# Gated cross-attention and routed experts on one core: the weights' low halves spread over the attention stage and beyond it, another order at the hand-off, and the second weight's exponential formed on ScalarE

## The chip, the cores and the metric
One Trainium2 chip, of which the kernel uses one core. The metric is the device time of one execution in microseconds (us); three executions of the kernel before took 288.73, 289.17 and 289.31, the median is 289.17. The profiled execution is a fourth.

## The reference
All in float32. x is 8 batches of 256 rows of 512; ctx is 8 batches of 256 rows of 512.

```python
def _layernorm(x): return (x - mean) / sqrt(var + 1e-5)

scores = einsum('bsd,bmd->bsm', layernorm(x), ctx) / sqrt(512)
scores = where(mask, scores, -1e30)
attn   = softmax(scores)
x = x + tanh(g_xattn) * where(any(mask), einsum('bsm,bmd->bsd', attn, ctx), 0)

xt    = layernorm(x).reshape(2048, 512)
probs = softmax(xt @ w_router.T)                # 8 experts
top_v, top_i = top_k(probs, 2); top_v /= sum(top_v)
g, u  = xt @ w_gate[e].T, xt @ w_up[e].T        # 192 columns each
out   = sum over the two experts of top_v * ((silu(g) * u) @ w_down[e].T)
x = x + tanh(g_ffn) * out
```

## The kernel before, in words
There are two stages on one core, with no pause between them.

**Attention.** The 2048 rows are cut into 16 tiles of 128 rows, numbered k, two per batch. A loop over steps s from 0 to 16 runs on every engine in the same form; each engine has its own queue, written out by hand, and semaphores join them. In step s TensorE transposes tile s (`t1`), transposes the attention weights of tile s-2 (`tp`), forms the scores of tile s-1 (`score`), the router's logits of tile s-4 (`rt`), the attention output of tile s-2 (`pv`) and transposes the second layernorm's output of tile s-3 (`t2`). VectorE in step s adds the attention output of tile s-3 to x (`x2`, the line X<-PO,rinv,X), takes the statistics of that sum, then those of the freshly loaded tile s+2 (`st1`), the row maximum of tile s-1 and the two bias columns. GpSimd raises the variances to the power -1/2 (`rstd`, rs<-mv) for both layernorms. ScalarE evicts, normalizes (XL and Y) and takes the exponentials.

Between these VectorE weaves the routing of each batch b: the two largest logits and their columns (`top2`), ranks among the rows of one expert (`ranks`), coefficients (`coefs`) and a table of slots (`slots`). Before, `top2` ends with dd = second maximum minus first, and `weigh` on ScalarE takes exp(dd).

**Weights.** 40 units of 128 by 512 or 64 by 512 numbers, numbered u: for expert e the parts n = 0, 1, 2 (gate and up), 3 (first 128 rows of down) and 4 (the last 64 rows of down). SyncE loads a unit (`loadw`), ScalarE rounds it to the high half (`hi`, semaphore s_wh), GpSimd subtracts to get the low half (`lo`, semaphore s_wl, the lines WGl<-WGl,WGh and so on). `SPLIT` says how many units each step takes. A unit with n = 4 is loaded into one of two buffers WS, so its load waits until the low half of the n = 4 unit two experts earlier is formed. SyncE's queue holds in one order the loads of x (`loadx`), of both forms of ctx (`loadct`, `loadcx`), of the weights and the stores of the routing coefficients: what stands behind a waiting load waits too.

**Experts.** The pairs (row, expert) are sorted by expert into 36 tiles of 128 rows that are run. The first NE = 9 of them come from batches 0 to 3 alone, so that their rows can be gathered before the attention is done. For tile j GpSimd gathers the rows (`gather`, XG<-x2s), TensorE transposes them (`tx`), multiplies with gate and up in three products of high and low halves (`gu`), transposes the product (`th`) and multiplies with down (`down`); ScalarE scales the result, and GpSimd scatters it with an addition into the output (out<-YT). `fence` and `landed` make a scatter wait for the one before it where the two may touch the same rows. TensorE waits before tile 0 until all 40 low halves are there.

## Time and profile before

| | |
|---|---|
| median of three executions | 289.17 us |
| the profiled execution | 288.54 us |
| its span, first to last instruction | 286.7 us |
| outside the span | 1.8 us |
| first `x2` of the attention starts | 18.50 us |
| last `x2` starts | 124.44 us |
| first expert product starts | 122.29 us |
| TensorE's mean granted clock | 0.973 |
| busy TensorE, VectorE, ScalarE, GpSimd | 87%, 62%, 52%, 58% |

A row of a timeline has the start and the duration in us, the engine and the line, then what is written from what, and in brackets the idle time of the engine before it with what ended it. Durations of neighbours on one engine overlap by about 0.1 us, since instructions are pipelined; the distance of two starts tells more than a sum of durations. A row of the windows has the stretch, its length, each engine's busy time with the number of instructions, the granted clock, the share in which the DMA engines were busy, and GB/s.

### The profile page before, as it was taken

To read this page: it belongs to the slowest core of one execution; us is meant where nothing else is said; L and a number is where in the kernel's file an instruction comes from. 1 tells how busy PE (TensorE), PEld (TensorE's weight loads), DVE (VectorE), ACT (ScalarE), POOL (GpSimd) and SP (SyncE) were. 2 spreads that over 40 slices of the span, in tenths; PEclk is the share of its full clock that TensorE was granted. 3 is DMA by queue.
4 is the path that set the end of the run, shared out by engine and by line. 5 is a ranking of instruction groups with operands and counts; after the bars stand their busy time and mean duration, and the time that the engine had idled before them with its cause. 6 is when DMAs were issued, how large, how long until landed. Compare 5 with 4: busy or idle time off the path is not lost.

```text
span 286.7 us, 5375 instructions
## 1 busy us (share of the span) xinstructions
PE 250.5 (87%) x1464; PEld 210.7 (73%) x1464; DVE 176.5 (62%) x645; ACT 149.9 (52%) x308; POOL 165.7 (58%) x153
## 2 busy tenths in 40 slices
PE   0999888988797878779999999999999999999940
PEld 0876666765575556459999889999999999999920
DVE  4465497999999799486586644454444454444420
ACT  3477977767585663154353445445445445444430
POOL 1267786567476465063632565648778875777440
PEclk9999999999999999798999999999999999999995
DMA  6999999988988321255543467459888999588753
GB/s 210 386 394 336 325 303 341 328 261 287 288 274 264 133 110 39 74 169 167 114 75 41 74 119 177 80 93 163 171 168 155 154 169 173 98 157 157 126 73 40
DMA packets 25951, 52.08 MB, mean 182 GB/s; under 512 B 5249, under 2 KB 5377, under 8 KB 25921
## 3 DMA queue, kind: packets, MB, share of 16 engines
q0 software_dynamic: 8304, 19.83, 37.8%
q1 hardware_dynamic: 13008, 23.50, 25.1%
q10 hardware_dynamic: 4608, 8.39, 7.7%
q8 instruction: 15, 0.25, 0.4%
q14 instruction: 16, 0.12, 0.2%
HBM read 33.81 MB, written 17.89 MB: 180 GB/s over the span
## 4 chain that ended last, share of the span: by engine, by line
PE 46%; DVE 21%; DMA 9%; issue 9%; POOL 8%; ACT 4%; ACTq 1%; POOLq 0%; DVEq 0%
PE S L1305 6%; PE S L1309 6%; PE S L1306 6%; DMA out<-YT,IXE 5%; PE A L1295 4%; DVE st L698 4%; PE PO L1154 3%; DVE X L739 3%; PE PO L1326 2%; PE PO L1331 2%; PE PO L1330 2%; PE PO L1327 2%; PE PO L1328 2%; DVE TB L805 2%; POOL WGl L407 2%
## 5 line engine op out<-in xcount | busy, mean ns | idle before, releaser
L1305 PE MATMUL S<-WGh,XTh 128*128 x144 | 52.1, 362 | 0.1
L1306 PE MATMUL S<-WGl,XTh 128*128 x144 | 48.8, 339 | 0.0
L398 POOL TENSOR_TENSOR rs<-mv,CS 128x1 f32<-128x1 f32 x32 | 17.8, 556 | 46.4 <-DVE mv L704 45.8
L492 POOL DMA_INDIRECT out<-YT,IXI x19 | 30.1, 1585 | 15.1 <-issue 5.7
L589 ACT ACTIVATE SG<-S 128x192 f32<-128x192 f32 x36 | 11.9, 332 | 49.0 <-PE S L1309 43.2
L1030 DVE TENSOR_TENSOR H<-SG,S 128x192 f32<-128x192 f32 x36 | 12.7, 354 | 39.7 <-ACT SG L589 34.7
L424 POOL DMA_INDIRECT XG<-x2s,IXG x30 | 29.5, 985 | 9.6 <-issue 5.5
L1154 PE MATMUL PO<-CX,PT 128*128 128x512 f32 x64 | 32.8, 637 | 2.5 <-DVE X L739 1.9
L407 POOL TENSOR_TENSOR WGl<-WGl,WGh 128x512 fp32r<-128x512 f32 x24 | 30.3, 1273 | 5.8 <-ACT WGh L570 5.6
L1309 PE MATMUL S<-WGh,XTl 128*128 x144 | 31.0, 337 | 0.0
L1143 PE MATMUL S<-CT,XLT 128*128 128x256 f32 x128 | 30.9, 385 | 0.0
L1023 DVE TENSOR_TENSOR XTl<-A,XTh 128x512 fp32r<-128x512 f32 x37 | 25.5, 690 | 8.1 <-ACT XTh L582 7.3
L582 ACT ACTIVATE XTh<-A 128x512 fp32r<-128x512 f32 x37 | 22.1, 599 | 11.3 <-PE A L1295 8.1
L1305 PEld LDWEIGHTS S<-WGh,XTh 128*128 128x128 f32 x144 | 27.5, 191 | 0.3 <-issue 0.2
L1306 PEld LDWEIGHTS S<-WGl,XTh 128*128 128x128 f32 x144 | 27.6, 192 | 0.0
L603 ACT ACTIVATE YT<-PO,cj 128x512 f32<-128x512 f32 x26 | 17.9, 688 | 17.7 <-PE PO L1331 13.1
L1036 DVE TENSOR_TENSOR HTl<-S,HTh 128x256 fp32r<-128x256 f32 x36 | 15.3, 424 | 18.7 <-ACT HTh L595 16.2
L1309 PEld LDWEIGHTS S<-WGh,XTl 128*128 128x128 f32 x144 | 25.6, 188 | 0.3 <-DVE XTl L1023 0.3
L1143 PEld LDWEIGHTS S<-CT,XLT 128*128 128x128 f32 x128 | 23.6, 195 | 2.9
L698 DVE BATCH_NORM_STATS2 st<-X 128x6 f32<-128x512 f32 x32 | 22.0, 689 | 4.3 <-DMA X<-in_x 3.6
L1295 PE MATMUL A<-CS,XG 128*128 128x128 f32 x148 | 22.7, 276 | 1.8 <-DMA XG<-x2s,IXE 1.7
L492 POOL DMA_INDIRECT out<-YT,IXE x7 | 11.2, 1594 | 19.1 <-DMA out<-YT,IXE 11.5
(168 smaller groups left out, 569.5 us busy)
## 6 DMA issues: line engine op xcount, KB each, us to landing
WGl<-in_wgu SPq DMA_DIRECT2D x24, 256.0 KB, 5.9
X<-in_x SPq DMA_DIRECT2D x16, 256.0 KB, 4.9
CT<-in_ctxt SPq DMA_DIRECT2D x8, 512.0 KB, 6.1
CX<-in_ctxn SPq DMA_DIRECT2D x8, 512.0 KB, 4.4
out<-X ACTq DMA_DIRECT2D x16, 256.0 KB, 4.9
x2s<-Y ACTq DMA_DIRECT2D x16, 256.0 KB, 3.9
WD1l<-in_wd SPq DMA_DIRECT2D x8, 256.0 KB, 5.4
WS<-in_wd SPq DMA_DIRECT2D x8, 256.0 KB, 5.3
```

The lines of the kernel that those rows point to most:

```text
L407: pool.tensor_tensor(out=low, in0=raw[p], in1=hi[p].bitcast(fp32), op=ALU.subtract).then_inc(s_wl, 1)
L424: pool.indirect_dma_start(out=XG[:, xg(j), :], out_offset=None, in_=rows, in_offset=bass.IndirectOffsetOnAxis(ap=at, axis=0))\
L492: pool.indirect_dma_start(out=out, out_offset=bass.IndirectOffsetOnAxis(ap=to, axis=0), in_=yt(j), in_offset=None, compute_op=ALU.add)\
L582: act.activation(XTh[:, j % 2, :, :], A0[:, :].rearrange("p (k c) -> p k c", k=KC), ACT.Copy).then_inc(s_xh, 1)
L698: n = mark(dve.bn_stats(st[:, k % 2, :], src))
L1023: dve.tensor_tensor(XTl[:, j % 2, :, :], A0[:, :].rearrange("p (k c) -> p k c", k=KC), XTh[:, j % 2, :, :].bitcast(fp32), ALU.subtract).th ...
L1143: m = pe.matmul(SC[k % 2][:, 0:S], XLT[:, k % 2, c, :], CT[:, b % 2, c, :], start=False, stop=(c == KC - 1))
L1154: m = pe.matmul(PO[:, :], PT[:, k % 2, c, :], CX[:, b % 2, c, :], start=(c == 0), stop=(c == 1))
L1295: m = pe.transpose(A0[:, 128 * c:128 * c + 128], XG[:, xg(j), 128 * c:128 * c + 128], ident)
L1305: pe.matmul(o, XTh[:, j % 2, c, :], WGh[:, bass.ds(e, 1), c, :], start=(c == 0), stop=False)
L1306: pe.matmul(o, XTh[:, j % 2, c, :], WGl[:, bass.ds(e, 1), c, :], start=False, stop=False)
L1309: m = pe.matmul(o, XTl[:, j % 2, c, :], WGh[:, bass.ds(e, 1), c, :], start=False, stop=(c == KC - 1))
```

## The change
It has five parts.

1. `SPLIT` becomes 1, 1, then two units in each of eleven steps, then 3, 4, 4, 5, where it was 1, 2, and then 3, 3, 2 repeated. Five units (u = 35 to 39) come behind the attention loop.
2. `UNITS` gives a new numbering: the n = 4 units of experts 4 and 5 are u = 20 and 21, those of experts 6 and 7 are u = 26 and 27, so that both WS buffers are free early for the expert stage. The wait of an n = 4 load is on the low half of that same buffer's last user.
3. In the loop, ScalarE's `hi` comes at the end of each step, GpSimd's `lo` runs one step later than `hi` and stands on both sides of the first `rstd`; SyncE's store of the coefficients stands ahead of the weights' loads.
4. At the hand-off GpSimd forms 11 low halves behind the loop, between and behind the first gathers. TensorE takes the expert numbers ahead of the last `pv`, `t2(14)` ahead of tile 0 and `t2(15)`, `rt(14)` behind it, and waits for each of the first five tiles only for the low halves that this tile uses. VectorE does `x2(15)` and its bias ahead of the first XTl; ScalarE takes `weigh(5)` and the last rows' normalization ahead of tile 0.
5. `weigh` takes exp(second maximum - first) straight from both maxima in two instructions, scale -1 and bias; VectorE's dd stays only for batches 6 and 7, whose power GpSimd takes.

```diff
-SPLIT = [0, 1, 2] + [3, 3, 2] * 4 + [3, 2]
-LATE = 5
+SPLIT = [0, 1, 1] + [2] * 11 + [3, 4, 4, 5]
+NA = sum(SPLIT[:NTK + 1])
+HEAD = 5
+UNITS = [(e, n) for e in range(4) for n in range(5)] + [(4, 4), (5, 4)] + [(4, n) for n in range(4)] \
+    + [(6, 4), (7, 4)] + [(e, n) for e in range(5, E) for n in range(4)]
...
-                if part(u)[1] == 4 and u >= 10:
-                    sp.wait_ge(s_wl, 5 * part(u)[0] - 5)
+                e, n = part(u)
+                if n == 4 and e >= 2:
+                    sp.wait_ge(s_wl, UNITS.index((e - 2, 4)) + 1)
...
             for s in range(NTK + 1):
-                if s <= LATE:
-                    for u in units(s - 1):
-                        lo(u)
+                for u in units(s - 1)[0:1]:
+                    lo(u)
                 if 0 <= s - 3:
                     rstd(mv2, s - 3, rs2, s_st2, s_rs2)
-                if s >= LATE:
-                    for u in units(s)[0:1]:
-                        lo(u)
+                for u in units(s - 1)[1:2 if s == NTK else NU]:
+                    lo(u)
                 if s + 2 < NTK:
                     rstd(mv1, s + 2, rs1, s_st1, s_rs1)
-                if s >= LATE:
-                    for u in units(s)[1:]:
-                        lo(u)
...
             gather(0)
+            for u in range(NA - 6, NA - 3):
+                lo(u)
             rstd(mv2, 14, rs2, s_st2, s_rs2)
...
+            lo(NA - 3)
             rstd(mv2, 15, rs2, s_st2, s_rs2)
             odds(6)
             stored(13)
             gather(3)
-            pool.wait_ge(s_tne, 1)
-            early = pool.value_load(TNE[0:1, 0:1], min_val=0, max_val=(1 << 13) - 1)
+            for u in range(NA - 2, NA):
+                lo(u)
             stored(14, 15)
             for j in range(4, NX):
                 gather(j)
+            for u in range(NA, NU):
+                lo(u)
+            pool.wait_ge(s_tne, 1)
+            early = pool.value_load(TNE[0:1, 0:1], min_val=0, max_val=(1 << 13) - 1)
...
-                act.wait_ge(s_dd, b + 1)
+                act.wait_ge(s_lc, b + 1)
...
-                act.activation(e2[:, :, :], dd[:, :, :], ACT.Exp).then_inc(s_e2, 1)
+                act.activation(e2[:, 0, :], mx[:, 0, 0:1], ACT.Exp, bias=mx[:, 0, 1:2], scale=-1.0)
+                act.activation(e2[:, 1, :], mx[:, 1, 0:1], ACT.Exp, bias=mx[:, 1, 1:2], scale=-1.0).then_inc(s_e2, 1)
...
-            side += [coefs(5), top2(6), taken()]
-            weave(queue(x2(14), first_xlo(), nbias(mv2, rs2, nb2, 14, s_rs2, s_nb2), x2(15)), 2)
+            side += [coefs(5)]
+            weave(queue(x2(14), nbias(mv2, rs2, nb2, 14, s_rs2, s_nb2)), 2)
+            side += [top2(6), taken()]
+            weave(queue(x2(15), nbias(mv2, rs2, nb2, 15, s_rs2, s_nb2), first_xlo()), 2)
...
-            pe.wait_ge(s_wl, NU)
             for j in range(NT):
                 with lives(pe, live, j):
+                    if j < HEAD:
+                        pe.wait_ge(s_wl, own[j] * 4 + 12)
+                    if j == HEAD:
+                        pe.wait_ge(s_wl, NU)
                     gu(j, own[j])
```

GpSimd's queue in step 12, before. rs2 is the second layernorm's factor (here of tile 9, then tile 10), rs1 the first one's (tile 14), the other rows are low halves.

```order
L398 TENSOR_TENSOR rs2<-mv2,CS 128x1 [waits s_st2]
L407 TENSOR_TENSOR WGl<-WGl,WGh 128x512 [waits s_wh]
L398 TENSOR_TENSOR rs1<-mv1,CS 128x1 [waits s_st1]
L407 TENSOR_TENSOR WD1l<-WD1l,WD1h 128x512 [waits s_wh]
L407 TENSOR_TENSOR WD2<-WS,WD2 64x512 [waits s_wl,s_wh]
L398 TENSOR_TENSOR rs2<-mv2,CS 128x1 [waits s_st2,s_wl]
```

The same place in the changed kernel, again from rs2 of tile 9 to rs2 of tile 10.

```order
L402 TENSOR_TENSOR rs2<-mv2,CS 128x1 [waits s_st2]
L411 TENSOR_TENSOR WD2<-WS,WD2 64x512 [waits s_rs2,s_wh]
L402 TENSOR_TENSOR rs1<-mv1,CS 128x1 [waits s_st1,s_wl]
L411 TENSOR_TENSOR WD2<-WS,WD2 64x512 [waits s_rs1,s_wh]
L402 TENSOR_TENSOR rs2<-mv2,CS 128x1 [waits s_st2,s_wl]
```

One low half fewer stands between the two, and the first WD2 row is now unit 19, the twentieth low half; the second is unit 20.

SyncE's queue ahead of the loads of x tiles 13 (semaphore s_so6), 14 (s_so0) and 15 (s_so1), before.

```order
L322 DMA X<-in_x 128x512 [waits s_y2,s_so6]
L339 DMA WGl<-in_wgu 128x512 [waits s_wh]
L339 DMA WD1l<-in_wd1 128x512 [waits s_wh]
L339 DMA WS<-in_wd2 128x512 [waits s_wl,s_wh]
L327 DMA CT<-in_ctxt 128x1024 [waits s_sc]
L322 DMA X<-in_x 128x512 [waits s_y2,s_so0]
L339 DMA WGl<-in_wgu 128x512 [waits s_wh] x3
L370 DMA x2s<-comb 256x1x8 [waits s_cb]
L332 DMA CX<-in_ctxn 128x1024 [waits s_pv]
L322 DMA X<-in_x 128x512 [waits s_y2,s_so1]
```

And in the changed kernel.

```order
L325 DMA X<-in_x 128x512 [waits s_y2,s_so6]
L343 DMA WS<-in_wd2 128x512 [waits s_wl,s_wh] x2
L330 DMA CT<-in_ctxt 128x1024 [waits s_sc]
L325 DMA X<-in_x 128x512 [waits s_y2,s_so0]
L372 DMA x2s<-comb 256x1x8 [waits s_cb]
L343 DMA WGl<-in_wgu 128x512 [waits s_wh] x2
L335 DMA CX<-in_ctxn 128x1024 [waits s_pv]
L325 DMA X<-in_x 128x512 [waits s_y2,s_so1]
```

Two loads into WS (units 20 and 21) stand one behind the other ahead of the load of x tile 14; the second of them waits for 20 low halves.

TensorE's queue at the hand-off, before: A0<-CS,XG is `tx`, A1<-CS,Y2 is `t2`, PL<-WR,Y2T is `rt`.

```order
L1154 MATMUL PO<-CX,PT 128x512
L1295 MATMUL A0<-CS,XG 128x128 [waits s_ere,s_inc,s_g0,s_eje,s_ixe]
L1295 MATMUL A0<-CS,XG 128x128 x3
L1171 MATMUL PL<-WR,Y2T 128x8 [waits s_y2t]
L1171 MATMUL PL<-WR,Y2T 128x8 x3
L1285 TENSOR_LOAD ERE
L1305 ISA [waits s_xh,s_wl]
```

And in the changed kernel.

```order
L1292 TENSOR_LOAD ERE [waits s_ere]
L1163 MATMUL PO<-CX,PT 128x512 [waits s_x2,s_cx1,s_pt]
L1163 MATMUL PO<-CX,PT 128x512
L1180 MATMUL PL<-WR,Y2T 128x8 [waits s_y2t]
L1180 MATMUL PL<-WR,Y2T 128x8 x3
L1302 MATMUL A0<-CS,XG 128x128 [waits s_inc,s_g0,s_eje,s_ixe]
L1302 MATMUL A0<-CS,XG 128x128 x3
L1171 MATMUL A1<-CS,Y2 128x128 [waits s_y2t,s_y2]
```

The expert numbers are read ahead of the last `pv`, and `t2(14)` stands ahead of tile 0's products, where it stood behind them.

## Rows read from the trace of the kernel before

**Rows 1.** Windows: attention steps 4 to 7, 8 to 14, 15 and 16, and the tiles.
```profile
22.94:49.26 26.32, 23.38 (x127) 17.08 (x126) 17.54 (x61) 20.68 (x43) 20.17 (x21) 1.00 0.97 324
49.26:99.56 50.30, 42.79 (x258) 31.82 (x256) 47.59 (x160) 34.30 (x70) 31.96 (x33) 1.00 0.81 267
99.56:116.43 16.87, 13.05 (x82) 9.64 (x80) 16.12 (x64) 8.85 (x19) 8.57 (x8) 1.00 0.22 70
175.00:274.00 99.00, 99.00 (x581) 90.84 (x579) 46.59 (x152) 47.61 (x102) 67.84 (x53) 1.00 0.79 143
```

**Rows 2.** VectorE's timeline, steps 10 and 11.
```profile
66.78 1.01 DVE L759 TENSOR_TENSOR dd<-mx 128x2 f32<-128x2 f32 x1
68.62 1.12 DVE L793 SCALAR_TENSOR_TENSOR rr<-Qi,sl 128x4 f32<-128x4 int32 x1
71.85 0.74 DVE L739 SCALAR_TENSOR_TENSOR X<-PO,rinv,X 128x512 f32<-128x512 f32 x1
73.97 0.69 DVE L698 BATCH_NORM_STATS2 st<-X 128x6 f32<-128x512 f32 x1
74.79 1.11 DVE L774 TENSOR_TENSOR Rt<-Rn,MS 128x8 bf16<-128x8 bf16 x1
...
78.20 0.74 DVE L739 SCALAR_TENSOR_TENSOR X<-PO,rinv,X 128x512 f32<-128x512 f32 x1
```

**Rows 3.** The same engine in step 8: dd with no low half beside it.
```profile
52.02 0.13 DVE L759 TENSOR_TENSOR dd<-mx 128x2 f32<-128x2 f32 x1
```

**Rows 4.** GpSimd's timeline, steps 10 and 11.
```profile
66.50 1.27 POOL L407 TENSOR_TENSOR WGl<-WGl,WGh 128x512 fp32r<-128x512 f32 x1
68.45 1.27 POOL L407 TENSOR_TENSOR WD1l<-WD1l,WD1h 128x512 fp32r<-128x512 f32 x1
69.86 1.73 POOL L407 TENSOR_TENSOR WD<-WS,WD 64x512 fp32r<-64x512 f32 x1
74.10 0.56 POOL L398 TENSOR_TENSOR rs<-mv,CS 128x1 f32<-128x1 f32 x1 [2.51 <-DVE mv L704]
74.62 1.27 POOL L407 TENSOR_TENSOR WGl<-WGl,WGh 128x512 fp32r<-128x512 f32 x1
```

**Rows 5.** SyncE's queue: timeline, then its waits (line, waited for: us, times, longest).
```profile
70.66 0.33 SPq L322 DMA_DIRECT2D X<-in_x  x1
85.97 0.33 SPq L339 DMA_DIRECT2D WS<-in_wd  x1
...
SPq L338 <- POOL WD L407: 4.6, 1, 4.6
```

**Rows 6.** The loads of x (line 322) by source: issue to landing, min/median/max.
```profile
DMA to landing us min/median/max: 2.7/4.9/7.5
```

**Rows 7.** Windows over the hand-off.
```profile
116.43:120.90 4.47, 3.58 (x6) 1.59 (x7) 1.44 (x3) 0.00 (x0) 0.00 (x0) 0.64 0.24 91
127.90:131.30 3.40, 3.40 (x22) 3.33 (x21) 2.42 (x10) 1.68 (x3) 1.20 (x3) 0.51 0.77 255
```

**Rows 8.** TensorE's timeline at the hand-off.
```profile
111.91 1.98 PE L1154 MATMUL PO<-CX,PT 128*128 128x512 f32 x4
117.32 3.38 PE L1154 MATMUL PO<-CX,PT 128*128 128x512 f32 x4 [1.93 <-DVE X L739]
127.55 0.78 PE L1295 MATMUL A<-CS,XG 128*128 128x128 f32 x4 [1.67 <-DMA XG<-x2s,IXE]
136.41 0.42 PE L1305 MATMUL S<-WGh,XTh 128*128 x1
```

**Rows 9.** VectorE's wait for `weigh(5)` at the hand-off.
```profile
122.17 0.17 DVE L811 TENSOR_SCALAR den<-e 128x2 f32<-128x2 f32 x1 [4.26 <-ACT e L576]
```

**Rows 10.** GpSimd's timeline, gathers, `odds` and scatters of the first tiles.
```profile
132.63 0.95 POOL L424 DMA_INDIRECT XG<-x2s,IXE  x1 [0.30 <-issue]
136.59 1.61 POOL L492 DMA_INDIRECT out<-YT,IXE  x1 [3.00 <-ACT YT L603]
144.99 0.73 POOL L416 TENSOR_TENSOR e<-CS,dd 128x2 f32<-128x2 f32 x1 [2.37 <-DVE dd L759]
145.97 1.67 POOL L492 DMA_INDIRECT out<-YT,IXE  x1 [0.25 <-ACT YT L603]
152.06 1.57 POOL L492 DMA_INDIRECT out<-YT,IXE  x1 [4.42 <-DMA out<-YT,IXE]
```

**Rows 11.** The chain of waits: start, us, what.
```profile
165.48 4.45 DMA XG<-x2s,IXG
169.97 0.66 PE A L1295 x4
```

More of the change, by code:

```diff
@@ L283, in part @@
         def part(u):
-            return u // 5, (u % 5 if u < NU - 5 else (u - 1) % 5)
+            return UNITS[u]
         def wunit(u):
@@ L364, in _ @@
                     loadx(s + 3)
-                for u in units(s + 2):
-                    loadw(u)
                 if s >= 9 and s % 2 == 1 and (s - 9) // 2 < B:
@@ L371, in _ @@
                                  comb[:, 2 * b:2 * b + 2, :]).then_inc(s_scb[b >= EB], 16)
+                for u in units(s + 2):
+                    loadw(u)
             live = tiles_of(sp)
@@ L412, in odds @@
             def odds(b):
-                pool.wait_ge(s_dd, b + 1)
+                pool.wait_ge(s_dd, b - 5)
                 pool.wait_ge(s_cb, b)
@@ L417, in odds @@
                     .then_inc(s_e2, 1)
+                last[0] = (s_e2, b + 1)
             def gather(j):
@@ L600, in yev @@
                 act.wait_ge(s_cj, j + 1)
+                if j == 5:
+                    act.wait_ge(s_wl, UNITS.index((7, 4)) + 1)
                 if j >= NB:
@@ L621, in _ @@
                     weigh((s - 7) // 2)
-                if s >= LATE:
-                    for u in units(s):
-                        hi(u)
                 if 0 <= s - 3 < NTK:
@@ L628, in _ @@
                     exp(s - 1)
-                if s < LATE:
-                    for u in units(s):
-                        hi(u)
+                for u in units(s):
+                    hi(u)
             ev2(13)
@@ L635, in _ @@
             evp(15)
-            xhi(0)
             weigh(5)
             act.activation(rsum[:, 0:1], rinv[:, 0:1], ACT.Silu)
+            for u in range(NA, NA + 2):
+                hi(u)
             store_x2(14)
             x2ln(14)
+            store_y2(14)
+            hi(NA + 2)
+            xhi(0)
+            ev2(14)
+            store_x2(15)
+            x2ln(15)
+            store_y2(15)
+            for u in range(NA + 3, NU):
+                hi(u)
             live = None
@@ L655, in _ @@
                     if j == 0:
-                        x2ln(15)
-                        store_y2(15)
+                        ev2(15)
                     if j >= 1:
@@ L746, in top2 @@
                 dve.wait_ge(s_rt, 2 * b + 2)
+                if b:
+                    dve.wait_ge(s_e2, b)
                 for i in range(2):
@@ L1095, in _ @@
                     mul(j)
-                    if j == 0:
-                        for _ in nbias(mv2, rs2, nb2, 15, s_rs2, s_nb2):
-                            pass
                     if j == AHEAD:
@@ L1332, in down @@
                     .then_inc(s_dn, 1)
+            tp(15)
+            pe.wait_ge(s_ere, 1)
+            own, live = experts(0, ERE, 0), None
+            pv(15)
+            rt(13)
             pe.wait_ge(s_ixe, 1)
@@ L1336, in _ @@
             pe.wait_ge(s_inc, 1)
-            pe.wait_ge(s_ere, 1)
             tx(0)
-            rt(13)
-            own, live = experts(0, ERE, 0), None
-            pe.wait_ge(s_wl, NU)
+            t2(14)
             for j in range(NT):
                 with lives(pe, live, j):
+                    if j < HEAD:
+                        pe.wait_ge(s_wl, own[j] * 4 + 12)
+                    if j == HEAD:
+                        pe.wait_ge(s_wl, NU)
                     gu(j, own[j])
-                    if j == 0:
-                        t2(14)
-                    if j == 1:
-                        t2(15)
-                        rt(14)
                     if j + 1 < NT:
@@ L1352, in _ @@
                     if j == 0:
+                        t2(15)
+                        rt(14)
                         cum(5)
```

13 lines of the change are left out of this document (2 added, 11 removed).

## The prediction
> **What bounds the kernel now.** I read the windows first. From 175 us to 274 us TensorE is busy in 99.00 of 99.00 us [rows 1]: the tiles run at TensorE's pace, and nothing in that stretch is changed. What can move is how early the tiles start and how smoothly the first ten run. In the attention the windows are cut at starts of `x2`. Steps 8 to 14 take 50.30 us, 7.19 each, with VectorE busy in 47.59 and TensorE in 42.79: VectorE sets the pace. Steps 4 to 7 take 26.32 us, 6.58 each, with TensorE at 23.38, VectorE at 17.54 and the DMA engines busy 0.97 of the time: there nobody is full, and the engines wait for GpSimd's factors, which stand behind low halves, and for loads.
>
> Then VectorE's timeline beside GpSimd's. The tiny dd takes 0.13 us alone [rows 3] and 1.01 us where a low half runs (66.50 to 67.77), rr takes 1.12 us under the next one, and Rt 1.11 us under the one at 74.62 [rows 2, 4]. So a low half of 1.27 us costs VectorE about 0.9 us. Step 10, with the three low halves at 66.50, 68.45 and 69.86, ends in the `x2` at 71.85; step 11, with two, runs from there to 78.20, 6.35 us [rows 2, 4].
>
> Taking dd away in six batches gives between its own 0.13 us and the 1.01 us of a stalled one each: 0.8 to 6.1 us. I take the low end, since the low half stays and other small instructions stand behind dd, as rr and Rt, which stalled as long.
>
> The Trainium skill (SBUF — State Buffer, Who interferes with whom) says that a VectorE instruction with two SBUF inputs contends with a GpSimd instruction that reads SBUF, and one of the two waits until the other is through. By this rule the next such instruction stalls in dd's place, and the low end is right; by the durations of dd alone the sum below would be up to 5.3 us lower.
>
> **The change part by part.**
>
> *Fewer low halves per step.* Steps 4 to 14 held 32 low halves and now hold 22; 6 of the 10 missing ones are in steps 8 to 14. If each of these seven steps takes the 6.35 us of step 11, they take 44.45 in place of 50.30: -5.9 us. The bounds: at TensorE's busy time per step (42.79 / 7 = 6.11) -7.5; if half of the gain goes to waits for TensorE and ScalarE, whose conversions now stand behind the exponential and ahead of the next evictions, -2.9. Steps 4 to 7 go from 3, 5, 3 and 3 low halves to 2 each. TensorE's own work there is 23.38 / 4 = 5.85 us a step; I take 6.1, between that and step 11: -1.9 (0 to -2.9). Steps 15 and 16 (16.87 us [rows 1]) keep three and two: 0. The 0.8 us of dd I count within this. `weigh` becomes two instructions for one and waits for the column search in place of dd; ScalarE has idle time for it: 34.30 busy in 50.30.
>
> *The wait that the new numbering makes.* The order of SyncE's queue shows two WS loads, units 20 and 21, ahead of the load of x tile 14. Unit 21 goes to the buffer of unit 19, so it waits for 20 low halves, and the twentieth stands in GpSimd's queue of step 12 behind the second layernorm's factor of tile 9. VectorE in the same step takes the statistics of tile 14 right behind those of tile 9. So VectorE now waits for a load that is issued only after its own work of this step. The path, from the start of `x2(9)`: 2.25 us to the start of the factor (71.85 to 74.10), 0.52 to the next row, about 0.15 for a WD2 unit's extra wait on GpSimd's own last result (an estimate from the 1.73 against 1.27 us at 69.86, which holds more than that), 1.27 for the low half: 4.2 [rows 2, 4]. Then WS, CT and x are issued one behind another, 0.33 us and a gap each: x tile 14 at 5.1. Before, the same load was issued at 70.66, 1.2 us before step 11 began [rows 5], over a step ahead of its use. Landing takes 4.9 us in the median, 2.7 to 7.5 [rows 6]: 10.0 (7.8 to 12.6). From those statistics to the next `x2` step 11 took 73.97 to 78.20, 4.2 us, of which I leave out one stall of 0.95 (Rt 1.11 against some 0.16), since the low half has passed during the wait: 3.3 (2.3 to 4.2). The step takes 13.3 us in place of 6.35: **+6.9** (+3.8 to +10.4). Queued behind the waiting x load's reader on VectorE are the bias of tile 9, the row maximum and the next `x2`, for which ScalarE and TensorE wait; no other engine's reserve covers it. Before, the longest wait of this kind in SyncE's queue was 4.6 us, and it stood behind the last x load [rows 5].
>
> TensorE idles some 7 us in that wait. At the hand-off an idle time of 1.93 us came ahead of a granted clock of 0.64, and one `pv` took 3.38 us in place of 1.98; after the idle 1.67 us the clock was 0.51, the 1.2 GHz level [rows 7, 8]. I add 0.2 us (0 to 1.7, half of a 3.40 us stretch): after the wait TensorE has slack against VectorE.
>
> The Trainium skill (TensorE: Matmul & The Clock Gate, The HAM clock gate) has the array start at half rate after it was idle. The rows agree; by that rule alone the whole 1.7 us would be paid, and the sum would be 1.5 us higher.
>
> *The hand-off.* Before, VectorE waited 4.26 us for `weigh(5)`, queued on ScalarE behind the first XTh [rows 9]; it now stands ahead. TensorE idles 1.67 us ahead of `tx(1)` for its gather, and gather 1 now goes out earlier, since the factor of tile 14 is ready about 4 us sooner. In exchange the first XTl comes behind the bias of tile 15, whose factor stands behind gathers 1 and 2 and a low half. Following the queues from `pv(15)` at 117.32 with TensorE's own work I get tile 2's product at about 132.5 in place of 136.41 [rows 8]: 3.9 us less. But that isn't paid out. Scatter 1 starts at 145.97, and the scatters and gather 10 hang on it one behind the other, until TensorE's transpose at 169.97 waits for that gather's landing [rows 10, 11]. GpSimd's queue up to scatter 1 now also holds two low halves ahead of gather 4 and five behind gather 5: gathers 4 and 5 end near 130.6 (worked out in this way) in place of 133.6, five times 1.27 leads to 137.0, the register load and scatter 0 follow at 137.8 (before 136.59), three gathers and `odds(7)` end at about 144.2, and scatter 1 starts at 144.5. So from tile 10 on the gain is 1.5 us, and the rest turns up as a wait of TensorE at tiles 9 and 10. That wait of about 2.4 us can drop the clock again (up to 1.7 us); I take 0.6 for it. Sum: **-0.9** (-3.9 to +1.7).
>
> **The sum.** -1.9 - 5.9 + 6.9 + 0.2 - 0.9 = -1.6 us. Against the profiled execution's own 288.54 (span 286.7 and 1.8 outside) that is 286.9; it lay 0.6 under the median of the runs, so against the median 289.17 - 1.6 = 287.6.
>
> **The rivals.**
>
> *The wait is short and the steps are quick.* x tile 14 lands in 2.7 us and the step pays 3.8; the other steps run at TensorE's pace (-7.5) and the scatter chain lets half of the hand-off through (-2.5): -1.9 - 7.5 + 3.8 - 2.5 = -8.1. With one or two of these true the time is about 283.5. For it: TensorE's busy time leaves this room [rows 1]. Against it: WS and CT, 0.75 MB together, are issued just ahead of x.
>
> *Slower: SyncE's queue decides.* The load of x tile 14 lands behind WS and CT only 7.5 us after its issue, and the wait costs +10.4 with the later statistics. The others give -8.7 + 0.2, so the kernel is slower as soon as the wait costs more than 8.5, which is a landing of 6.5 us; with clock losses of 1.5 it comes to +3.4: 292.5. For it: the DMA share in steps 8 to 14 is 0.81 and loads of x have taken 7.5 us. Against it: with fewer weights the queues are emptier.
>
> *The low halves don't set VectorE's step.* The stalls are then paid by whichever instruction comes, and the seven steps stay near 7 us: -1.9 - 1.3 + 6.9 - 0.9 + 0.2 = +3.0, 292.2. For it: step 11 follows a step in which TensorE had run ahead, so its 6.35 may be a recovery. Against it: rows 2 and 4 put each stall under a low half.
>
> *The exponential doesn't do what it says*: ScalarE's two instructions relieve VectorE by no more than 0.13 us each time. That is the low end that I took, and lies within the first case.
>
> **How the numbers follow.** Forecast 0.45 (287.6, own range 285.5 to 290), short wait 0.25, slow queue 0.18, steps as before 0.12. A measurement of this kernel can tell about 0.2%, 0.6 us. In the first case 0.68 is faster, 0.18 within, 0.14 slower: 0.31, 0.08 and 0.06. With the others: faster 0.56, within 0.09, slower 0.35. The range reaches from the middle of the second case to the middle of the slow ones: 282.5 to 292.5.
>
> **What would show it.** In the attention one step of 11 to 15 us, with VectorE idle 5 us or more before the statistics of a loaded tile, released by the load X<-in_x, and in SyncE's queue a wait on a WD low half of some 10 us; around it steps of 6.1 to 6.6 us. `den` at the hand-off without the 4 us of idle time. TensorE waiting for XG at tile 9 or 10. If no such load wait is there, the second term is wrong; if the steps stay above 6.9 us, the first is; if scatter 1 moves as much as tile 2, the third is.

## The result and the profile after

The changed kernel takes 299.27 us in the median (4 runs, 298.73 to 299.87), beside 289.24 us (288.73 to 290.41, 4 runs) for the kernel before on the same chip: ratio 1.034 (95% interval 1.030 to 1.038). It is 10 us slower, where 1.6 us less was forecast, and lies above the range. The profiled execution has a span of 297.2 us, before 286.7. Here and below a median is that of all runs of a kernel, while a ratio and its 95% interval leave out the runs that took over 1.5% longer than the fastest of their kernel.

First the windows of the kernel after, cut as in [rows 1] at starts of `x2`, with the tiles (the experts' stage), and last the hand-off from `x2(13)` to tile 3's product, followed by the same stretch of the kernel before (columns: stretch, its length, busy time of PE, PEld, DVE, ACT, POOL, granted clock, DMA share, GB/s).

```profile
23.14:46.93 23.79, 22.62 (x127) 17.10 (x126) 16.46 (x61) 18.06 (x39) 14.35 (x16) 1.00 0.91 308
46.93:99.52 52.59, 44.46 (x258) 33.20 (x256) 37.23 (x155) 33.28 (x72) 25.95 (x28) 0.94 0.68 234
175.00:274.00 99.00, 99.00 (x583) 91.14 (x582) 45.98 (x151) 47.65 (x101) 69.85 (x56) 1.00 0.79 146
107.98:151.97 43.99, 34.79 (x165) 28.50 (x164) 35.02 (x113) 17.86 (x35) 28.34 (x26) 0.73 0.42 117
```
```profile
108.23:142.48 34.25, 29.33 (x171) 23.91 (x170) 23.23 (x112) 13.72 (x27) 15.49 (x16) 0.90 0.42 114
```

Steps 4 to 7 take 23.79 us (before 26.32), steps 8 to 14 52.59 (50.30), and `x2(15)` starts at 124.27 as before at 124.44. The tiles from 175 us on are as they were. The hand-off takes 43.99 us in place of 34.25: +9.7, nearly the whole loss. TensorE is busy 5.5 us more in it, with nearly the same matmuls at a granted clock of 0.73 in place of 0.90, and idle 9.2 us in place of 4.9. VectorE is "busy" 11.8 us more (35.02 against 23.23) with 113 instructions against 112.

The wait that was forecast in the attention, on SyncE's queue (timeline, then its waits), on GpSimd (the twentieth low half) and on VectorE, which answers to [rows 5], [rows 4] and [rows 2]:

```profile
58.92 0.33 SPq L325 DMA_DIRECT2D X<-in_x  x1
61.25 15.22 SPq L343 DMA_DIRECT2D WS<-in_wd  x2
76.52 0.42 SPq L330 DMA_DIRECT2D CT<-in_ctxt  x1
77.03 0.38 SPq L325 DMA_DIRECT2D X<-in_x  x1
...
SPq L342 <- POOL WD L411: 25.5, 4, 14.5
```
```profile
74.80 1.26 POOL L411 TENSOR_TENSOR WD<-WS,WD 64x512 fp32r<-64x512 f32 x1
```
```profile
72.16 0.74 DVE L748 SCALAR_TENSOR_TENSOR X<-PO,rinv,X 128x512 f32<-128x512 f32 x1
81.12 0.69 DVE L707 BATCH_NORM_STATS2 st<-X 128x6 f32<-128x512 f32 x1 [6.94 <-DMA X<-in_x]
87.67 0.75 DVE L748 SCALAR_TENSOR_TENSOR X<-PO,rinv,X 128x512 f32<-128x512 f32 x1 [3.22 <-PE PO L1163]
```

The second WS load waits 14.5 us, the load of x tile 14 goes out at 77.03, VectorE idles 6.94 us for it, and the step takes 72.16 to 87.67, 15.5 us. The other six steps take 37.1 us, 6.18 each.

Now the hand-off. VectorE's timeline with its three longest rows (TB is two instructions):

```profile
113.78 4.75 DVE L815 TENSOR_SCALAR TB<-CS,rr 128x128 fp32r<-128x128 f32 x2
...
128.34 3.19 DVE L957 TENSOR_TENSOR pn<-CS,inc 128x16 f32<-128x16 f32 x1
...
134.62 5.49 DVE L1053 TENSOR_TENSOR cj<-XG,EJ 128x8 f32<-128x8 f32 x1
140.14 0.16 DVE L1054 TENSOR_REDUCE cj<-cj 128x1 f32<-128x8 f32 x1
```

And GpSimd's in the same places, ten of the eleven low halves behind the loop, with gather 0 ahead of the first three:

```profile
112.71 1.74 POOL L429 DMA_INDIRECT XG<-x2s,IXE  x1 [0.52 <-DVE IXE L920]
114.48 2.50 POOL L411 TENSOR_TENSOR WGl<-WGl,WGh 128x512 fp32r<-128x512 f32 x2
116.94 1.25 POOL L411 TENSOR_TENSOR WD1l<-WD1l,WD1h 128x512 fp32r<-128x512 f32 x1
...
128.96 2.53 POOL L411 TENSOR_TENSOR WGl<-WGl,WGh 128x512 fp32r<-128x512 f32 x2
...
133.87 1.30 POOL L411 TENSOR_TENSOR WD1l<-WD1l,WD1h 128x512 fp32r<-128x512 f32 x1
135.11 3.75 POOL L411 TENSOR_TENSOR WGl<-WGl,WGh 128x512 fp32r<-128x512 f32 x3
138.83 1.25 POOL L411 TENSOR_TENSOR WD1l<-WD1l,WD1h 128x512 fp32r<-128x512 f32 x1
```

`pn` reads 16 columns and `cj` 8, and both last until the row of low halves on GpSimd is through (131.49 and 140.08). TensorE waits 3.73 us for the `x2` behind TB and 3.33 us for the HTl behind `cj`, and runs at the lower clock after each:

```profile
120.41 3.75 PE L1163 MATMUL PO<-CX,PT 128*128 128x512 f32 x4 [3.73 <-DVE X L748]
130.21 1.48 PE L1316 MATMUL S<-WGh,XTl 128*128 x4
135.63 0.87 PE L1316 MATMUL S<-WGh,XTl 128*128 x4
140.97 0.50 PE L1337 MATMUL PO<-WD1h,HTl 128*128 x1 [3.33 <-DVE HTl L1046]
146.03 1.48 PE L1316 MATMUL S<-WGh,XTl 128*128 x4
```

Where [rows 8] had tile 2's product start at 136.41, its part with XTl (137.89 then) starts at 146.03. One clock loss lies ahead of all eleven low halves: `pv(14)` at 111.69 took 3.48 us, 1.98 before [rows 8]; it made nobody wait, since the next `x2` came only behind TB.

### The profile page after: what moved, and what is told of

The parts are those of the page before. It is cut to its first block, busy times and chain, and to the rows that moved or that the text cites. A ratio compares the mean times of both kernels' runs of the same rounds, so it can differ in the third digit from the quotient of the medians.

```text
span 297.2 us, 5387 instructions
## 1 busy us (share of the span) xinstructions
PE 258.2 (87%) x1464; PEld 217.7 (73%) x1464; DVE 176.8 (59%) x639; ACT 150.6 (51%) x314; POOL 165.8 (56%) x153
## 4 chain that ended last, share of the span: by engine, by line
PE 69%; DVE 16%; issue 5%; POOL 3%; DMA 2%; ACT 2%; SPq 0%; ACTq 0%; POOLq 0%; DVEq 0%
PE S L1312 9%; PE S L1316 9%; PE S L1313 9%; PE PO L1163 7%; PE A L1302 6%; PE S L1152 5%; DVE TB L815 3%; PE PO L1333 3%; PE PO L1338 3%; PE PL L1180 3%; PE PO L1337 3%; PE PO L1334 3%; PE PO L1335 3%; PE S L1323 3%; DMA X<-in_x 2%
## 5 line engine op out<-in xcount | busy, mean ns | idle before, releaser
L1312 PE MATMUL S<-WGh,XTh 128*128 x144 | 53.1, 369 | 0.0
L1313 PE MATMUL S<-WGl,XTh 128*128 x144 | 49.8, 346 | 0.0
L1163 PE MATMUL PO<-CX,PT 128*128 128x512 f32 x64 | 36.4, 697 | 3.7 <-DVE X L748 3.7
L1316 PE MATMUL S<-WGh,XTl 128*128 x144 | 32.2, 346 | 0.0
L1312 PEld LDWEIGHTS S<-WGh,XTh 128*128 128x128 f32 x144 | 28.1, 195 | 0.6 <-issue 0.4
L1313 PEld LDWEIGHTS S<-WGl,XTh 128*128 128x128 f32 x144 | 28.3, 196 | 0.0
L1316 PEld LDWEIGHTS S<-WGh,XTl 128*128 128x128 f32 x144 | 26.8, 196 | 0.0
L1180 PEld LDWEIGHTS PL<-WR,Y2T 128*128 128x128 f32 x128 | 18.5, 213 | 10.5 <-issue 10.0
L572 ACT ACTIVATE Y<-X,nb,rs 128x512 f32<-128x512 f32 x16 | 13.0, 812 | 24.2 <-DVE nb L722 24.0
```

Of the source, the lines that this page charges most:

```text
L1163: m = pe.matmul(PO[:, :], PT[:, k % 2, c, :], CX[:, b % 2, c, :], start=(c == 0), stop=(c == 1))
L1180: m = pe.matmul(PL[:, 8 * i:8 * i + 8], Y2T[:, c, :], WR[:, c, :], start=(c == 0), stop=(c == KC - 1))
L1312: pe.matmul(o, XTh[:, j % 2, c, :], WGh[:, bass.ds(e, 1), c, :], start=(c == 0), stop=False)
L1313: pe.matmul(o, XTh[:, j % 2, c, :], WGl[:, bass.ds(e, 1), c, :], start=False, stop=False)
L1316: m = pe.matmul(o, XTl[:, j % 2, c, :], WGh[:, bass.ds(e, 1), c, :], start=False, stop=(c == KC - 1))
```

## The experiments

Theory A: the wait for x tile 14 costs what it shows. Theory P: the eleven low halves that GpSimd forms behind the attention's loop cost the hand-off its 10 us, because VectorE's instructions wait for them. The rivals to P: GpSimd's queue time (Q), and the new order of tiles 14, 15 and 0 (O).

**e1: the wait.** Unit 21 is loaded into a part of the weights that is still free, so nothing waits for the twentieth low half.

```diff
-                return wd2[e], WS[:, e % 2, :], WD2[:, e, :], WD2[64:128, e, :]
+                raw = WD1l[:, 7, :].bitcast(fp32) if e == 5 else WS[:, e % 2, :]
+                return wd2[e], raw, WD2[:, e, :], WD2[64:128, e, :]
...
```


> The changed kernel, but unit 21 (the last 64 rows of expert 5's down weights) is loaded into the still unused place of unit 39 in WD1l, not into the WS buffer of unit 19, so the load of x tile 14 has nothing to wait behind. Theory A (the wait on the twentieth low half makes the 15.5 us step and all of it is paid): step 12 comes down to 6.4 us and the kernel to about 290.2 us, 9.1 less than the changed kernel. Rival (the loss sits at the hand-off alone, and the attention's wait is given back there): under 3 us less, 296 or more, although the step is short.

290.62 us (10 runs), ratio 1.008 (1.005 to 1.011). The step from 71.98 takes 6.82 us and steps 8 to 14 43.9:

```profile
71.98 0.75 DVE L751 SCALAR_TENSOR_TENSOR X<-PO,rinv,X 128x512 f32<-128x512 f32 x1
78.80 0.74 DVE L751 SCALAR_TENSOR_TENSOR X<-PO,rinv,X 128x512 f32<-128x512 f32 x1
```

The step is 8.7 us shorter than in the changed kernel; the time falls by 8.65 us between the medians and by 7.5 between the ratios (1.034 and 1.008). A is shown. The hand-off is still slow (43.7 us), with the longest instruction of VectorE in it:

```profile
124.70 6.43 DVE L1056 TENSOR_TENSOR cj<-XG,EJ 128x8 f32<-128x8 f32 x1
```

All kernels below but e2, e4 and e8b have this edit.

**e2 and e3: gaps.** Ahead of every low half GpSimd waits for its own last result.

```diff
-                if half:
-                    settle()
+                settle()
                 pool.tensor_tensor(out=low, ...)
```


> The changed kernel, but every low half on GpSimd first waits for GpSimd's own last result, which leaves a gap of some 0.15 us between two low halves in a row. Theory B (low halves issued back to back keep the shared port for the whole run, and VectorE's 4.75, 3.19 and 5.49 us instructions at the hand-off are that): each of the three falls to 1.4 us or less, TensorE's idle time of 3.3 us in tile 0's down product goes, and the kernel takes about 291 us, 8 less than the changed kernel. Rival C (low halves behind a gather hold VectorE up whatever the gap, since the long ones all stand behind an indirect DMA): the three stay above 3 us and the time stays within 1 us of 299.3. The 15.5 us step stays in both.

> Both edits together. Theories A and B together: 299.3 - 9.1 - 8 = about 282 us, faster than the kernel before by 7. With A and rival C: 290. With the rival of A and B: 288 to 291.

e2: 297.32 us, ratio 1.029 (1.023 to 1.035); e3: 288.29, 0.999 (0.996 to 1.002). In e2 two pieces of TB take 2.32 us in place of 4.75 and `pn` 1.96 in place of 3.19; `cj` is through before its row (0.15), and in its place Qi takes 1.78, TA 1.50 and four pieces of TB 3.00 (1.11 in the changed kernel). TB and `pn` miss the 1.4 us expected, and the gain is only about 2 us, not 6 to 8: a gap lets an instruction in, and later ones wait again.

**e4: the exponential alone**, in the kernel before.

```diff
-                act.activation(e2[:, :, :], dd[:, :, :], ACT.Exp).then_inc(s_e2, 1)
+                act.activation(e2[:, 0, :], mx[:, 0, 0:1], ACT.Exp, bias=mx[:, 0, 1:2], scale=-1.0)
+                act.activation(e2[:, 1, :], mx[:, 1, 0:1], ACT.Exp, bias=mx[:, 1, 1:2], scale=-1.0).then_inc(s_e2, 1)
...
```


> The kernel before with the fifth part of the change alone: exp(second maximum - first) in two ScalarE instructions straight from both maxima, dd only for batches 6 and 7. Theory (another instruction stalls in dd's place): within 1 us of the kernel before, 288.2 to 289.2 us. Rival (dd's stalls are saved): the 2.4 us that dd took over its shortest in six batches and more go, 286.5 us or less.

290.67 us (12 runs from 287.32 to 293.90), ratio 1.005 (1.001 to 1.009): no gain, rather a small loss. The low end is right. In its trace dd is gone from step 10, and TA behind it now takes 1.61 us, where the kernel before had dd at 1.01 and rr at 1.12 and TA at 0.68; step 10 is 0.3 us shorter for it and step 11 0.3 longer.

**e5b, e6b, e7b: moving low halves.** e5b puts the three low halves behind gather 0 behind tile 14's factor and gathers 1 and 2. e6b spreads the last five over gathers 6 to 8 and tiles 1 and 2. e7b does both.

```diff
             gather(0)
-            for u in range(NA - 6, NA - 3):
-                lo(u)
             rstd(mv2, 14, rs2, s_st2, s_rs2)
+            lo(NA - 6)
...
             for j in range(4, NX):
                 gather(j)
-            for u in range(NA, NU):
-                lo(u)
...
                     for g in GATHERS[j]:
                         gather(g)
+                        if g < 9:
+                            lo(NA + g - 6)
```


> As e1_spare, and the three low halves behind gather 0 stand behind the factor of tile 14 and behind gathers 1 and 2, where VectorE waits for TensorE. Theory D (VectorE's step 16 took 11.5 us in place of 8.2 because three low halves ran while it formed tables with two-input instructions): step 16 takes 8.2 us again, 287.3 us, 3.3 less than e1_spare. Rival (the blocked instructions are only shifted and block the next stretch as long): 290 to 291.

> As e1_spare, but the last five low halves stand one behind each of gathers 6, 7 and 8 and one each in tiles 1 and 2, and TensorE waits per tile for what it uses up to tile 8. Theory D (five in a row behind gather 5 hold VectorE for 6.4 us in tile 0, TensorE idles 4 us and its clock falls): the distance of tiles 1 and 2 falls from 11.0 to about 6 us, 284.5 us, 6 less than e1_spare. Rival (the order of the hand-off itself is what is slow): at most 1 us less, 289.6 or more.

> Both moves together on e1_spare. Theory D: 290.6 - 3.3 - 6 = 281.3 us, faster than the kernel before by some 7 us. The rivals: 287 or more.

e5b: 290.0 us, 1.006 (1.001 to 1.010). Step 16 falls from 11.5 us in e1 to 7.4, but tile 0 starts no earlier: VectorE waits for tile 15's factor, now behind the moved low halves.

```profile
117.88 0.21 DVE L726 TENSOR_SCALAR nb<-mv,rs 128x1 f32<-128x1 f32 x1 [4.13 <-POOL rs L405]
```

e6b: 287.68 us, 0.996 (0.991 to 1.000), 3 us less than e1 where 6 were expected. Tiles 1 and 2 are 4.8 us apart in place of 11.0, as expected, but tiles 4 and 5 are 8.3 apart in place of 4.4. One piece of TB is held beside the low half that now follows the scatter of tile 1, and TensorE waits behind it:

```profile
140.83 2.58 DVE L820 TENSOR_SCALAR TB<-CS,rr 128x128 fp32r<-128x128 f32 x1
```
```profile
143.55 0.19 PE L1199 MATMUL PC<-MS,CB 128*128 128x8 bf16 x1 [2.21 <-DVE MS L783]
```

e7b: 287.86 us, 0.988 (0.979 to 0.997), from 4 runs of 285.12 to 292.09; 281.3 was expected, and by the medians it is no faster than e6b. In e5b and e6b the place that a low half is moved to costs part of what the old one did.

**e8b: the other way.** The kernel before with five added GpSimd subtractions of two SBUF inputs (464 columns, results unused) behind gather 5.

```diff
+            for o in (PXb[:, 0:464], PXb[:, 464:928], YT[:, 2, 0:464], YT[:, 3, 0:464], YT[:, 4, 0:464]):
+                pool.tensor_tensor(out=o, in0=CS[:, 0:464], in1=CS[:, 61:525], op=ALU.subtract).then_inc(s_px, 1)
```


> The kernel before with five more GpSimd subtractions of 464 columns with two SBUF inputs behind gather 5, whose results nobody reads (1.15 us each by the 1.27 us of 512 columns). Theory D: one VectorE instruction with two SBUF inputs takes 4 us or more, the distance of tiles 1 and 2 grows from 6.05 us by 3 or more, and the kernel takes 292 to 295 us. Rival (the reordering of ScalarE, VectorE and TensorE at the hand-off made the loss): within 1 us of the kernel before.

290.52 us, 1.005 (1.002 to 1.009). The block is there, on VectorE and GpSimd (the profiled run took 294.19 us, 3.7 above the median, so only its pattern is read):

```profile
135.00 5.55 DVE L770 TENSOR_TENSOR OH<-CS,ix 128x32 f32<-128x32 f32 x1
```
```profile
135.65 1.97 POOL L482 TENSOR_TENSOR past_x<-CS 128x464 bf16<-128x464 f32 x2
137.58 2.93 POOL L482 TENSOR_TENSOR YT<-CS 128x464 f32<-128x464 f32 x3
```

Tiles 1 and 2 are 8.1 us apart, before 6.05: 2.0 more, where 3 were expected. Alone, five such instructions cost about 1.5 us of the whole and not 3 to 6. How much of a block reaches the end hangs on the place; by itself this run does not tell P from O, the next ones do.

**e9, e13, e14: how much, and by what.** In e9 the eleven low halves are cut to one subtraction of 8 columns; in e13 each is six of them in a row; in both the other columns are left out, so these two kernels tell about time alone. In e14 each is whole, in eight subtractions of 64 columns.

```diff
-                pool.tensor_tensor(out=low, in0=raw[p], in1=hi[p].bitcast(fp32), op=ALU.subtract).then_inc(s_wl, 1)
+                n, w = (6, 8) if u >= NA - 6 else (1, w)      # e9: (1, 8), e14: (8, 64)
+                for i in range(n):
+                    c = slice(w * i, w * i + w)
+                    ins = pool.tensor_tensor(out=low[:, c], in0=raw[p][:, c], in1=hi[p].bitcast(fp32)[:, c], op=ALU.subtract)
+                ins.then_inc(s_wl, 1)
```


> The kernel with the spare buffer (e1), in which GpSimd's low halves of the units from the 29th on (eleven of them, all behind the loop) are cut to 8 columns of 512 each, in the same places, with the same semaphores and the same order of everything on every engine; the rest of their columns is left out of the computation. e1: 290.6 us, tile x2(13) at 99.1, tile 3's product at 142.8, so 43.7 us against 34.3 in the kernel before. Theory P (the low halves' work in the hand-off costs the time, by blocking VectorE's instructions): the instructions of 4.75, 3.2 and 6.4 us fall below 2 us, x2(13) to tile 3 takes 34 to 37 us, and the time is 282 to 285 us. Rival O (the new order in the hand-off, tile 15's bias ahead of tile 0's low half, costs most of it whatever the low halves do): the long instructions fall, but x2(13) to tile 3 still takes over 40 us, and the time is 287.5 to 290 us.

> The kernel with the spare buffer (e1), in which each of the eleven low halves behind the loop is done as six subtractions of 8 columns in a row on GpSimd (e9 has one of them; 0.2 to 0.25 us each in its trace), so that GpSimd's queue is taken for about 1.3 us as by a whole low half, but by short instructions; the rest of the columns is left out of the computation. e1: 290.6 us, e9: 277.4 us. Theory P (the loss of e1 is VectorE's instructions blocked by long ones of GpSimd, and the queue time of GpSimd costs little): the time stays at 277 to 281 us, with no VectorE instruction over 2 us from tile 14 on. Rival Q (the loss is GpSimd's queue: the factors of tiles 14 and 15 and the gathers stand behind the low halves for as long): 286 to 291 us, with short VectorE instructions.

> The kernel with the spare buffer (e1), with nothing left out: each of the eleven low halves behind the loop is done whole by GpSimd, as eight subtractions of 64 columns in a row. Each should take 0.2 to 0.4 us, so a low half 1.6 to 3 us against 1.27. If what blocks VectorE is the length of one instruction on GpSimd (P, released between any two): VectorE's instructions from tile 14 on stay under 2 us, and the time is 280 to 287 us. If GpSimd keeps VectorE out through a row of instructions without a gap, or the queue time costs the same (Q): 291 to 297 us, with VectorE's instructions of 4 us and more in the first case.

e9: 277.36 us, ratio 0.960 (0.952 to 0.969), 13 us less than e1 and even less than P had. The windows of e1 and of e9 from `x2(13)` to tile 3:

```profile
99.09:142.81 43.72, 30.30 (x165) 24.88 (x164) 35.79 (x113) 17.73 (x35) 28.28 (x26) 0.84 0.42 117
```
```profile
100.98:129.85 28.87, 24.66 (x164) 20.86 (x164) 22.52 (x113) 17.41 (x35) 17.05 (x26) 1.00 0.62 170
```

The low halves cost 14.85 us there, of which 5.6 are TensorE's busy time at the lower clock (30.30 against 24.66) and 9.2 its idle time. With them gone the new hand-off is 5.4 us shorter than the old one's 34.25, so rival O is out.

e13: 276.65 us, ratio 0.958 (0.950 to 0.966). GpSimd's queue is taken by the subtractions for 11.6 us, by the whole low halves of e1 for 13.8, and it costs nothing over e9: rival Q is out for a queue time of this size. GpSimd and VectorE in e13, where `cj` of tile 1 passes inside the row (in e1 the `cj` of tile 0 took 6.43 us):

```profile
120.55 1.54 POOL L418 TENSOR_TENSOR WD1l<-WD1l,WD1h 128x8 fp32r<-128x8 f32 x6
122.06 2.97 POOL L418 TENSOR_TENSOR WGl<-WGl,WGh 128x8 fp32r<-128x8 f32 x18
125.00 1.00 POOL L418 TENSOR_TENSOR WD1l<-WD1l,WD1h 128x8 fp32r<-128x8 f32 x6
```
```profile
123.15 0.15 DVE L1061 TENSOR_TENSOR cj<-XG,EJ 128x8 f32<-128x8 f32 x1
```

e14: 289.42 us, ratio 1.002 (0.997 to 1.006): between its two cases, and a little under e1's. A low half takes 2.25 us in pieces, a row of 16 pieces holds one instruction of VectorE for 3.80 us and one of 40 pieces for 4.09. But this run mixes P and Q: the pieces take GpSimd's queue for 25.1 us, and in tile 4 VectorE waits 2.88 us for a result of GpSimd that stands behind them (last row below).

```profile
121.05 4.49 POOL L418 TENSOR_TENSOR WGl<-WGl,WGh 128x64 fp32r<-128x64 f32 x16
```
```profile
121.21 3.80 DVE L975 SCALAR_TENSOR_TENSOR jq<-sv,bad 128x1 f32<-128x1 f32 x1
...
145.67 0.17 DVE L829 TENSOR_SCALAR den<-e 128x2 f32<-128x2 f32 x1 [2.88 <-POOL e L428]
```

**e10 and e11: the old order** of VectorE, ScalarE and TensorE in the hand-off, put back in e1 and in e7b.

```diff
-            side += [coefs(5)]
-            weave(queue(x2(14), nbias(mv2, rs2, nb2, 14, s_rs2, s_nb2)), 2)
-            side += [top2(6), taken()]
-            weave(queue(x2(15), nbias(mv2, rs2, nb2, 15, s_rs2, s_nb2), first_xlo()), 2)
+            side += [coefs(5), top2(6), taken()]
+            weave(queue(x2(14), first_xlo(), nbias(mv2, rs2, nb2, 14, s_rs2, s_nb2), x2(15)), 2)
...
```


> The kernel with the spare buffer (e1), with all low halves where they are, but the order of VectorE, ScalarE and TensorE in the hand-off (from tile 14's normalisation to tile 1's product) put back to the one of the kernel before: the low half of tile 0's rows right behind x2(14), tile 15's bias behind the first product, tile 0's high half ahead of ScalarE's last weights. Theory P (low halves): tile 0 may start 1 to 3 us earlier, but the row of low halves blocks VectorE as before, at other instructions; 288.5 to 291 us. Rival O (the order costs most of it): the first product starts 4 us earlier or more, and the time is 284 to 287.5 us.

> The kernel of e7b (spare buffer, three low halves behind tile 14's factor, five low halves spread behind later gathers and tiles), with the order of VectorE, ScalarE and TensorE in the hand-off put back to the one of the kernel before, as in e10. e7b: 287.9 us, tile 0's low half at 119.1, 3.6 us behind a wait on tile 15's factor. If what is left of the loss is tile 0 standing behind tile 15's factor (theory PO): tile 0's low half at 114 to 116, 283 to 285.5 us, the fastest kernel so far and faster than the one before. If what is left comes from the low halves wherever they stand (P alone): 286.5 to 288.5 us.

e10: 296.16 us (4 runs), 1.022 (1.009 to 1.036); e11: 291.32, 1.009 (1.005 to 1.014). Both are slower than with the new order, by 5.5 and 3.5 us of the medians, and both expectations missed: the part of tile 0 with XTl does start at 114.6 in e11, but that of tile 1 follows 12.9 us later. In the old order `den` stands behind ScalarE again, so the factor of tile 14 and gather 1 behind it come late, and TensorE waits for that gather:

```profile
112.91 0.17 DVE L828 TENSOR_SCALAR den<-e 128x2 f32<-128x2 f32 x1 [4.91 <-ACT e L590]
```
```profile
120.46 1.11 PE L1310 MATMUL A<-CS,XG 128*128 128x128 f32 x4 [3.62 <-DMA XG<-x2s,IXE]
```

Then two instructions of VectorE take 1.92 and 2.92 us beside low halves, and TensorE waits 1.89 us for H. So the old order has a price of its own, and the low halves block in it as well.

**e12 and e15: VectorE forms the low halves**, behind HTl of tiles 0 to 8. Nothing is left out; it holds for inputs whose tiles up to the eighth need experts 0 to 4 alone.

```diff
                     steps(SIDES[j][2])
+                    for u in range(NA - 6 + vl(j), NA - 6 + vl(j + 1)):
+                        dve.wait_ge(s_wh, u + 1)
+                        dve.wait_ge(s_wl, u)
+                        _, raw, hi, low = wunit(u)
+                        dve.tensor_tensor(low, raw, hi.bitcast(fp32), ALU.subtract).then_inc(s_wl, 1)
...
```


> The kernel with the spare buffer (e1), in which the eleven low halves behind the loop are whole again, but formed by VectorE, not GpSimd: one behind the low half of H of each tile from 0 to 8, two in tiles 5 and 6; nothing is left out of the computation. It relies on the order of this input's tiles (experts 5 to 7 first needed from tile 9 on). VectorE's nearest row, the low half of a tile's rows (128x512, one operand from PSUM), is 0.68 us, and VectorE is idle 1.1 to 1.3 us in each of the tiles behind the third; e9 (GpSimd's low halves cut to nothing) has 277.4 us, ratio 0.960. Theory P (GpSimd's low halves cost 13 us by blocking VectorE, the subtractions themselves nearly nothing where VectorE does them): 277.5 to 280.5 us, ratio 0.96 to 0.97, no instruction of VectorE over 2 us from tile 14 on, tiles 0 to 8 at 3.9 to 5.4 us each. Rival V (what is saved on GpSimd comes back as time of VectorE, 11 times 0.7 to 1.3 us on the path): 285 to 290 us, tiles 0 to 8 0.7 to 1.3 us longer each than in e9.

> The kernel of e12 (spare buffer, the eleven low halves behind the loop formed by VectorE, nothing left out), with the two low halves that stood in tile 5 put into tiles 7 and 8: one each in tiles 0 to 4, none in tile 5, two each in tiles 6 to 8. In e12's trace the two low halves at 149.88 and 150.66 stood ahead of the product H of tile 6; TensorE waited 2.08 us for it (0.68 in e9), the granted clock fell to the 1.2 GHz level, and the distance from tile 6 to tile 7 was 8.64 us against 6.05 in e9. Where this placement is what e12 pays over e9: that distance is about 6.1 us again, and the time is 277 to 281 us by the median, ratio 0.955 to 0.97, the fastest whole kernel. Rival (VectorE's 11 low halves cost wherever they stand, or e12's loss lies in the half clock that it showed at pv(15), 3.78 us against 1.96, ahead of any of them): 281 to 285 us by the median as e12, with a wait of TensorE of 2 us on VectorE at tile 7 or 8, or the half clock at pv(15) again.

e12: 283.2 us (6 runs, 278.3 to 286.3; before 289.6), e15: 281.24 (278.1 to 283.3; before 289.13). The ratios are 0.965 (0.961 to 0.969, from 2 of the 6 runs) and 0.968 (0.962 to 0.974, from 4); by the medians of all runs they are 0.978 and 0.973, and by its median e12 lies in the gap between its two cases. Every run of both is faster than every run of the kernel before. The profiled runs took 284.55 and 283.32 us. In e12 two low halves stand ahead of H of tile 6 (VectorE, then TensorE):

```profile
149.88 0.68 DVE L1123 TENSOR_TENSOR WGl<-WGl,WGh 128x512 fp32r<-128x512 f32 x1
150.66 0.69 DVE L1123 TENSOR_TENSOR WD1l<-WD1l,WD1h 128x512 fp32r<-128x512 f32 x1
151.27 0.35 DVE L1036 TENSOR_TENSOR H<-SG,S 128x192 f32<-128x192 f32 x1
```
```profile
151.81 0.44 PE L1327 MATMUL S<-CS,H 128*128 128x128 f32 x2 [2.08 <-DVE H L1037]
```

The distance of tiles 6 and 7 was 8.64 us; with the two low halves moved it is 6.24 in e15. But now TensorE waits for the last ones ahead of tile 9, and `pv(15)` ran at the lower clock again (3.78 us against 1.96 in e9), ahead of any of VectorE's low halves:

```profile
108.96 3.78 PE L1167 MATMUL PO<-CX,PT 128*128 128x512 f32 x4 [0.63 <-ACT PT L546]
161.03 0.44 PE L1316 MATMUL S<-WGh,XTh 128*128 x1 [2.78 <-DVE WD1l L1123]
```

So both halves of e15's expectation came true in part. A subtraction takes 0.68 us on VectorE and 1.27 on GpSimd, where it stops VectorE too. These are the fastest kernels of the study that leave nothing out.

## Why the prediction was wrong, step by step

- **Steps 4 to 7, -1.9:** measured -2.5 (23.79 against 26.32), within its bounds.
- **Steps 8 to 14, -5.9:** the six undisturbed ones took 6.18 us each, where 6.35 was taken; against 7.19 before that is -7.0 for seven. Right as a time; the rival of unchanged steps fell. The count was turned round: of the ten low halves that left steps 4 to 14, four left steps 8 to 14 (18 became 14) and six left steps 4 to 7. Four times the 0.9 us read from [rows 2, 4] is 3.6, so this price explains half of the gain; the other half is not worked out.
- **The wait, +6.9:** right in place, cause and signature (6.94 us of idle time released by X<-in_x). The step took 15.5 us, not 13.3: +9.3 over 6.18. The load went out 4.9 us behind the start of the step (77.03 - 72.16; 5.1 was worked out), and landed 4.1 us later, nearer to the median of 4.9 than to either bound. What was missed is behind the statistics: 6.6 us to the next `x2` (81.12 to 87.67), not 3.3, since the granted clock had fallen to 0.52 there (`pv` took 3.76 us in place of 1.96) and `x2` waited 3.22 us for TensorE. The 0.2 for the clock belongs to this: the clock that was lost over the idle time was paid. The rule of the Trainium skill (TensorE: Matmul & The Clock Gate, The HAM clock gate), by which the array starts at half rate after it was idle, was the better guide, and the sum by it only 1.5 us nearer.
- **The exponential, 0:** right (e4). The upper bound of 6.1 us was too high by the rows of before: dd took 1.01 us in two of its six batches, 0.61 and 0.26 in two and 0.13 in two, 2.4 us over its shortest in all.
- **The hand-off, -0.9 (-3.9 to +1.7):** measured +9.7. This is the step that failed, and its error of 10.6 us is nearly all of the forecast's 11.6. The prediction priced the eleven low halves as time in GpSimd's queue alone (five times 1.27 ahead of scatter 1) and moved VectorE along as if GpSimd were idle. e9 shows that the eleven cost 13 us of the whole, and e13 that this is not their queue time but what they do to VectorE: it waits for them, TensorE waits for it, and then runs at half rate. The same rows that gave 0.9 us of VectorE for each low half [rows 2, 4] gave a warning: eleven times 0.9 is 9.9 us, on an engine for which TensorE waits there [rows 8]. The price was read in the attention and never charged where the low halves went. That 9.9 lies near the 9.7 measured is chance: the low halves cost 14.85 us there, and the new order gave 5.4 back.
- Inside the failed step the part on the order was right: with the low halves out (e9) the stretch to tile 3 is 5.4 us shorter than before, and `den` no longer waits. In e9 TensorE has no wait over 0.4 us at tiles 9 and 10 either, and scatter 1 starts 12.6 us earlier than before (133.33 against 145.97), as much as the product of tile 3 (129.85 against 142.48): that the gain "isn't paid out" was not borne out there.
- **The rivals:** the first three dealt with the attention, the first with the scatters too. The attention's net came out as it stood in the sum within a microsecond (-0.7 forecast with the wait, about -0.2 measured). None put a price on the hand-off's low halves, so the range ended 7 us too low. The chances of the cases add up to 0.36 for slower and 0.08 for within, where 0.35 and 0.09 stand.

The Trainium skill (SBUF — State Buffer, Who interferes with whom) says that of an instruction of VectorE with two SBUF inputs and one of GpSimd that reads SBUF one waits until the other is through. The prediction let it decide whose stall went away and not where it came back. The traces agree that VectorE waits, but the rule read for one instruction understates the matter: `cj` waited through a row of five low halves, 5.49 us, not through one of 1.25.

## What to carry to other kernels

Work that is moved off a full stretch keeps its price: look for what it did to its neighbours in the old place, and charge that in the new one, per instruction, before following any queue. Here a subtraction of 512 columns on GpSimd took VectorE's time too, so it is free only where VectorE has nothing to do; where both are wanted, VectorE did it in half the time (0.68 us against 1.27). And a chain that hangs between two engines should be priced with the clock: TensorE's idle times of 3.73 and 3.33 us at the hand-off were each followed by matmuls at half rate, and against e9 the 9.2 us of idle time in e1 came with 5.6 us of slower matmuls.
